# Graph kernel on one core: a shorter segment-maximum recurrence, and node blocks moved from the second graph stage beside the softmax tail of the output stage

## The reference, cut to what matters

```python
logits = w1[target] - w2[source] + d
seg_max = jax.ops.segment_max(logits, target, num_segments=m)
e = jnp.exp(logits - seg_max[target])
denom = jax.ops.segment_sum(e, target, num_segments=m)
out = jax.ops.segment_sum(e / denom[target] * (w3[source] + d), target, num_segments=m)
```

## Time and profile before

| | us |
|---|---|
| median of 3 runs (3369.0 to 3388.23) | 3370.6 |
| profiled execution | 3347.96 |
| its span, first to last instruction | 3346.2 |
| busy: PE, DVE, POOL, ACT | 2459.9, 2486.4, 1925.5, 1724.2 |

### The profile page before, as it was taken

One profiled execution on the slowest core, in us unless ns is written; L12 is line 12 of the kernel. 1 busy time (PEld: TensorE's weight loads), 2 busy tenths in 40 slices (PEclk: granted clock), 3 DMA queues, 4 the chain that ended last, 5 costly groups with the idle time before them and its releaser, 6 DMA issues. The chain is left out here.

```text
span 3346.2 us, 53978 instructions
## 1 busy us (share of the span) xinstructions
PE 2459.9 (74%) x14171; PEld 1675.7 (50%) x14171; DVE 2486.4 (74%) x4558; ACT 1724.2 (52%) x3950; POOL 1925.5 (58%) x1870
## 2 busy tenths in 40 slices
PE   3976666666578789979946779998999998995000
PEld 1543444444467667745525556665666656663000
DVE  5569999999777758859966747776566665888553
ACT  3784444444222258858841126665566655775221
POOL 4008888887488800068870047775655437886776
PEclk9988787787777888879977989998999998997555
DMA  4133333433466668733313445555445543332111
GB/s 129 64 96 87 107 99 107 109 106 98 119 199 196 191 144 180 153 104 115 112 46 75 113 127 167 157 162 159 135 136 141 139 106 108 112 114 68 47 47 27
DMA packets 742887, 393.28 MB, mean 118 GB/s; under 512 B 517090, under 2 KB 649265, under 8 KB 742770
## 3 DMA queue, kind: packets, MB, share of 16 engines
q1 hardware_dynamic: 691582, 333.94, 36.4%
q0 software_dynamic: 51200, 58.03, 6.8%
HBM read 217.18 MB, written 175.64 MB: 117 GB/s over the span
## 5 line engine op out<-in xcount | busy, mean ns | idle before, releaser
L1341 POOL DMA_INDIRECT g_W<-t,g_cols x400 | 463.2, 1158 | 260.8 <-PE g_pS L2901 116.4
L460 POOL DMA_INDIRECT fr_W<-in_x,fr_idx x400 | 496.0, 1240 | 127.6 <-issue 107.7
L1341 POOL DMA_INDIRECT me_W<-t,me_cols x200 | 236.0, 1180 | 58.0 <-issue 46.9
L1341 POOL DMA_INDIRECT ou_W<-t,ou_cols x200 | 222.6, 1113 | 58.1 <-issue 40.8
L3433 POOL DMA_INDIRECT de_V<-t,de_cols x200 | 215.8, 1079 | 53.6 <-issue 41.4
L3117 POOL DMA_INDIRECT out<-ou_F,ou_ways x200 | 200.1, 1000 | 77.5 <-issue 53.3
L1058 PE MATMUL at_pL<-at_XF,w_logit 128*128 128x512 f32 x100 | 89.7, 996 | 123.0 <-ACT at_XF L1105 123.0
L1331 POOL COPY g_cols<-pos 128x8 int32 (+1 forms) x50 | 19.8, 396 | 241.2 <-POOLq L85 241.0
L1331 POOL COPY de_cols<-pos 128x8 int32 (+1 forms) x25 | 8.1, 324 | 261.4 <-POOLq L85 261.2
L931 ACT ACTIVATE me_nzt<-me_pXT 128x512 f32<-128x512 f32 x47 | 28.1, 598 | 170.9 <-PE me_pXT L914 170.9
L914 PE MATMUL at_pXT<-ident,at_nz 128*128 128x128 f32 x200 | 40.3, 336 | 93.8 <-ACT at_nzt L931 52.3
(11 more groups left out here) (619 smaller groups left out, 8536.8 us busy)
## 6 DMA issues: line engine op xcount, KB each, us to landing
mg_y<-wanted SPq DMA_DIRECT2D x50, 256.0 KB
at_nx<-in_x SPq DMA_DIRECT2D x50, 256.0 KB, 2.6
x<-at_nz SPq DMA_DIRECT2D x50, 256.0 KB, 3.3
x1T<-at_nzt SPq DMA_DIRECT2D x50, 256.0 KB, 2.9
t<-up_X SPq DMA_DIRECT2D x100, 128.0 KB, 2.0
t<-g_HS SPq DMA_DIRECT2D x50, 256.0 KB
t<-g_HD SPq DMA_DIRECT2D x50, 256.0 KB, 3.4
g_D<-t SPq DMA_DIRECT2D x50, 256.0 KB
```

What stands on the lines that cost most here:

```text
L460: self.nc.gpsimd.indirect_dma_start(out=self.W[w][b][:, (2 * t + h) * C:(2 * t + h + 1) * C], out_offset=None, in_=self.table, in_offset=b ...
L1341: nc.gpsimd.indirect_dma_start(out=slot(w, b, t), out_offset=None, in_=table, in_offset=bass.IndirectOffsetOnAxis(ap=cols[w][:, c:c + 1], ...
```

## The change

Four parts.

1. **Attention.** The mask goes into the recurrence one edge ahead: `M = max(M_before, pL) + anew`, with `anew` read from `same` one column further on (the tile gets two more columns, set to zero). A single DVE difference `A = M_before - pL` is left. ACT makes the two exponents from it, as `L = Relu(A)` and `A = Relu(-A)`, and takes `Exp` with scale -1 of both.
2. **Node blocks.** BLOCKS_G1 is 21, gcn2_stage has none and its steps follow `by_ring`, and output_stage has 47: 25 beside its edge steps and 22 beside the tail (`LateOrder`). The order is turned round: the dense stage does blocks 0 to 28 and the last one, the output stage 50 to 96.
3. **Tail.** Each operation on G3 handles a whole step in one instruction, on 128x512. `late` weaves it between the node lane's operations. The norm is written back into G3, and POOL copies it from there into F before it scatters.
4. **Scatter.** POOL no longer waits for all node blocks, but for as many as the last target row of the step needs. That number is worked out on DVE at the head of the stage (`needed`) and loaded into a register per step. x3 is loaded by one DMA a step, the first two ahead of the stage's other loads.

```diff
-                        s.activation(anew[b][:, :], k.same[:, bass.ds((2 * q + b) * CE, CE)], ACT.Copy,
+                        s.activation(anew[b][:, :], k.same[:, bass.ds((2 * q + b) * CE + 1, CE)], ACT.Copy,
...
+                    for b in first:
+                        act.wait_ge(e["diffs"], last_of(q, b))
+                        s.activation(L[b][:, :], A[b][:, :], ACT.Relu).then_inc(e["bent"], 1)
+                        s.activation(A[b][:, :], A[b][:, :], ACT.Relu, scale=-1.0).then_inc(e["bent"], 1)
                     for b in second:
                         act.wait_ge(e["zcen"], last_of(r, b))
...
-                        v.tensor_tensor_scan(M[b][:, 1:CE + 1], anew[b][:, :], pL[b][:, :], M[1 - b][:, CE:CE + 1],
-                                             ALU.add, ALU.max).then_inc(e["maxed"], 1)
+                        v.tensor_tensor_scan(M[b][:, 1:CE + 1], pL[b][:, :], anew[b][:, :], M[1 - b][:, CE:CE + 1],
+                                             ALU.max, ALU.add).then_inc(e["maxed"], 1)
                         dve.wait_ge(e["maxed"], last_of(q, b))
+                    for b in first:
+                        v.tensor_tensor(A[b][:, :], M[b][:, 0:CE], pL[b][:, :], ALU.subtract)\
+                            .then_inc(e["diffs"], 1)
...
-                    for b in first:
-                        v.tensor_tensor(L[b][:, :], pL[b][:, :], M[b][:, 1:CE + 1], ALU.subtract)
-                        v.tensor_tensor(A[b][:, :], M[b][:, 0:CE], anew[b][:, :], ALU.add).then_inc(e["shifted"], 1)
-                    for b in first:
-                        dve.wait_ge(e["shifted"], last_of(q, b))
-                        v.tensor_tensor(A[b][:, :], A[b][:, :], M[b][:, 1:CE + 1], ALU.subtract)\
-                            .then_inc(e["diffs"], 1)
```

The counts and the scatter:

```diff
-BLOCKS_G1, BLOCKS_G2, BLOCKS_OU = 23, 22, 23
+BLOCKS_G1, BLOCKS_OU = 21, 47
+FIRST_OU = D_FULL - BLOCKS_OU
+FIRST_G1 = FIRST_OU - BLOCKS_G1
...
                 def scatter(q, w):
                     pool.wait_ge(sent, q + 1)
+                    pool.wait_ge(e["norm"], q + 1)
+                    if again(q):
+                        for b in range(2):
+                            pool.wait_ge(scattered[w][b], ring_count(q, w, 16 * CT) - 16 * CT)
+                    nc.gpsimd.tensor_copy(F[w][:, :], G3[:, bass.ds(q * (G * C), G * C)]).then_inc(copied, 1)
+                    blocks = nc.gpsimd.value_load(needed[0:1, bass.ds(q, 1)], min_val=16, max_val=16 * BLOCKS_OU)
+                    pool.wait_ge(lane.o_out, blocks)
+                    pool.wait_ge(copied, q + 1)
                     for b in range(2):
-                        pool.wait_ge(e["norm"], last_of(q, b))
...
-                beside.stored(pool)
+                pool.wait_ge(told, 8)
```

The tail on ACT and its place among the lane's operations (DVE and PE are woven alike):

```diff
+                def late(f, w, x, y, z):
+                    if x is not None:
+                        lane.act_relu(act, x)
+                        lane.act_square(act, x)
+                    if y is not None:
+                        lane.act_flat3(act, y)
+                    if z is not None:
+                        lane.act_exp(act, z)
+                    soft(f)
+                    if y is not None:
+                        lane.act_hidden(act, y)
...
+                    squares(f)
...
+                    spread(f)
+
+                beside.run_late(act, step, late)
```

More of the change, by code:

```diff
@@ L274, in _ @@
                 gp.memset(k.w_value[:, 0:C], 0.0)
+                gp.memset(k.same[:, EP:EP + 2], 0.0)
                 gp.memset(k.ones[:, :], 1.0)
@@ L2871, in step @@
                         own_rows(q + 2, w)
-                    beside.load(sp, q + 2, w)
                     store(q)
-                    beside.store(sp, q - 2, out)
                 for q in range(2):
                     own_rows(q, q, used=False)
-                    beside.load(sp, q, q)
-                beside.run_queue(sp, step)
-                beside.stored(sp)
+                with sp.Fori(0, ITERS // 2 - 1) as j:
+                    step(2 * j, 0)
+                    step(2 * j + 1, 1)
+                for q in range(ITERS - 3, ITERS):
+                    step(q, q % 2)
                 for b in range(2):
@@ L3386, in _, with top @@
-                beside.run(dve, step)
-                by_two(dve, finish)
+                part = lambda f: groups(G3[:, bass.ds(f * (G * C), G * C)], G)
+                def top(f):
+                    dve.wait_ge(e["kept"], 2 * f + 2)
+                    v.tensor_reduce(out=st[:, 0, :], in_=part(f), op=ALU.max, axis=AX).then_inc(e["max"], 1)
+                    dve.wait_ge(e["max"], f + 1)
+                    reuse(dve, e["norm"], f)
+                    v.tensor_tensor(O4, part(f), over(st[:, 0, :], C), ALU.subtract).then_inc(e["less"], 1)
@@ new lines, in by_degree, with total @@
+                def by_degree(f):
+                    dve.wait_ge(e["less"], f + 1)
+                    v.tensor_tensor(O4, O4, over(k.dinv[:, bass.ds(f * G, G)], C), ALU.mult).then_inc(e["scaled"], 1)
+                def total(f):
+                    dve.wait_ge(e["exp"], f + 1)
+                    v.tensor_reduce(out=st[:, 1, :], in_=O4, op=ALU.add, axis=AX).then_inc(e["esum"], 1)
+                    dve.wait_ge(e["esum"], f + 1)
+                    v.reciprocal(st[:, 2, :], st[:, 1, :]).then_inc(e["erec"], 1)
@@ new lines, in norm, with late @@
+                def norm(f):
+                    dve.wait_ge(e["dev"], f + 1)
+                    v.tensor_tensor(part(f), O4, over(st[:, 4, :], C), ALU.mult).then_inc(e["norm"], 1)
+                def late(f, w, x, y, z):
+                    if z is not None:
+                        lane.dve_max(dve, z)
+                        lane.dve_less(dve, z)
+                    top(f)
+                    if x is not None:
+                        lane.dve_clamp(dve, x)
+                    by_degree(f)
+                    if z is not None:
+                        lane.dve_esum(dve, z)
+                        lane.dve_recip(dve, z)
+                        lane.dve_soft(dve, z)
+                        lane.dve_mix4(dve, z, w)
+                    total(f)
+                    if x is not None:
+                        lane.dve_scale(dve, x)
+                        lane.dve_mix2(dve, x, w)
+                    mix(f, 1 - w)
+                    if z is not None:
+                        lane.dve_sumsq4(dve, z)
+                    if x is not None:
+                        lane.dve_sumsq2(dve, x)
+                    if z is not None:
+                        lane.dve_norm4(dve, z)
+                    sumsq(f)
+                    if x is not None:
+                        lane.dve_norm2(dve, x, w)
+                    norm(f)
@@ L3390, in dense_stage @@
+                v.tensor_copy(needed[:, :], whole[:, :]).then_inc(told, 1)
+                beside.run_late(dve, step, late)
 def dense_stage(nc, k, out):
```

330 lines of the change are left out of this document (157 added, 173 removed).

## The result

The changed kernel takes 3281.6 us (median of 4 runs, 3265.6 to 3292.3) against 3371.8 for the kernel before (4 runs beside them, 3369.0 to 3388.2): a ratio of 0.9715, 95% interval 0.9682 to 0.9749. Run again beside the first experiments it gave 3300.6 against 3372.8, ratio 0.9761 (0.9687 to 0.9834). The forecast of 3287 us lies between the two. The profiled execution has a span of 3263.9 us, 82.3 less than before; the sum had said 84.

The account below looks back on a forecast made before the run. It took DVE to bound attention, PE the second graph stage and scatters the old tail. Terms -29 - 4 - 133 + 2 + 80 = -84 us, taken off the runs' median 3370.6, gave 3287 us; range 3225 to 3360.

Parts of the forecast that it names:

- the sum: Whole kernel: the stage terms added up, -84 us against the profiled 3348.0 us.
- Attention, -29 forecast: Attention: four fewer DVE instructions save 2.41 us a step, a new wait costs 1.2; step 23.7 instead of 24.87.
- The walk through one step: Attention: following DVE and ACT from the scans' end, four Relus delay ACT's square and DVE waits some 1.2 us.
- Case A: Attention: POOL's gathers keep the step at 24.9 us, no gain there, total 3316 us; chance 0.15.
- gcn1, -4 forecast: First graph stage: two steps lose their node work and get 2 us shorter each; bounds 0 and 4.
- gcn2, -133 forecast: Second graph stage: without its 22 node blocks, 22 steps of 17.24 us become 11.2, paced by POOL's gathers.
- the bound of -100: Second graph stage: steps of 12.7 us if PE's clock falls with its load, a gain of only 100 us.
- Output stage, +82 forecast: Output stage: +2 us in the first part, +80 in the tail, with 22 tail steps of 13.9 us.
- the two terms: Output tail, DVE's step: 12.4 us of work plus 1.5 of waits, 13.9 us together.
- Case B: Output tail: scatters held by DVE's two-input instructions pace it at 16.5 us a step, total 3344 us; chance 0.18.
- Case C: Output tail: node and softmax chains do not overlap, 20.8 us a step, total 3438 us; chance 0.09.

Follow-up runs that it names:

- the first experiments: The first of three series of follow-up runs, with the kernel before run beside it at a median of 3372.8 us.
- the merged tail alone: The kernel before with its softmax tail's DVE and ACT instructions covering both halves of a step, no node block moved: 3379.5 us, ratio 1.0028.
- the halves: The changed kernel with each of DVE's nine softmax instructions in the tail issued as two of half the size: 3299.3 us, ratio 0.9793.
- two more copies: The changed kernel with two more 128x512 copies on POOL in each tail step, into tiles nobody reads: 3284.2 us, ratio 0.9713.
- the second execution: The changed kernel run again unchanged and profiled: 3300.6 us, ratio 0.9761; its profile is 37.1 us longer than the first.

## Why the prediction was right

**What bounds each stage.** All four readings held: DVE in attention, PE in gcn2, scatters in the old tail (shown by the merged tail alone), DVE in the new tail (shown by the halves; with two more copies POOL still kept up). For gcn2 the reading was right but one figure was not: by subtraction of the node lane's tiles, PE was to have 8.8 us a step left, and it has 10.

**Attention, -29 forecast, -34.9 measured.** The walk through one step named the new wait, its place (DVE's reduce of R) and its cause (the Relus ahead of ACT's square). Its size was 0.82 us, not 1.2: the Relus start 0.52 us apart and not 0.60. So the step gained 1.5 us instead of 1.2, and the steps after the first are the miss. Moving the Relus took the wait away, which shows the cause.

**Case A** (gathers hold attention at 24.9) is out: 23.4 in the changed kernel, 22.7 with the Relus early. POOL is busy 441 us in the stage instead of the 472 of the earlier trace rows, as its gathers are held less.

**gcn1, -4 forecast, -19.5 measured.** Mis-sized, and partly no effect of the change. "Two steps get 2 us shorter" was too little here: the last four scans (of the first half of a step) come 11.9, 12.6, 9.8 and 8.6 us apart, before 14.2, 14.0, 11.9 and 12.6, so 9.8 us less for two blocks, and what follows the last scan takes 3.5 us instead of 5.9. Another 6.2 us are two steps of the kernel before that took 17.2 us instead of 14.1, because the clock fell in them. The step before it and that step:

```profile
2090.00:2104.00 14.00, 14.00 (x90) 9.56 (x89) 10.95 (x17) 9.42 (x19) 10.95 (x10) 1.00 0.61 170
2104.00:2122.00 18.00, 18.00 (x94) 11.92 (x94) 11.38 (x19) 10.46 (x22) 9.70 (x10) 0.81 0.53 143
```

With the attention change alone there is no such step, and gcn1 takes 359.1 us instead of 365.9; the changed kernel has none in one execution and one in the other. The end of the stage varies as well: in the second execution the last two intervals are 10.6 and 12.1 us, at a granted clock of 0.87 and 0.50 (0.65 and 0.80 in the first), so the four lost only 5.5 us, near the forecast's 4. One more us was not looked into.

**gcn2, -133 forecast, -135.1 measured.** Step 11.0, not 11.2; late next was the gather, as read from the head of the old stage. PE waits for gathered tiles, as here between 2380 and 2530 us, where POOL has little but its issue gaps:

```profile
PE g_pS L2939 <- DMA g_W<-t,g_cols: 13.9, 13, 1.1
```

The clock did not fall (0.96 over the stage), so the bound of -100 was not needed. But PE's load did not fall as said either: 10.0 us of a step of 11.0, not 8.8 of 11.2. The subtraction took no account of times that overlap: the other tiles already held PE 155.4 of the 252.5 us of the earlier trace rows, 10.6 a step. By these numbers 1 us more would have made PE set the step. In the second execution the stage took 299 us, with steps of 11.4 and gathers of 1100 ns instead of 1052: 125 us less than before.

**Output stage, +82 forecast, +88.7 measured.** From the stage's start the first norm comes after 320.5 us (316.4 by the sum), then 22 steps of 14.01 in the mean (13.9), then 47.7 us to the end of the span (47.5). In the step shown above the two terms were off in opposite directions: DVE's work is 12.66 us (12.4), its waits 1.04 (1.5), and the only wait that the profile names is norm4's, 0.60. PE's part is 8.4 only at a granted clock of 1.00, and 9.9 at the usual 0.88. POOL's comes to 12.8, from its copy to the end of its last scatter (12.1). Seventeen of the 22 steps are 13.4 to 13.9; the rest are steps in which the clock was 0.77 to 0.86, or the very last, at 0.51. In the second execution the mean is 14.35, with nine steps of 14.9 to 15.8.

**Case B** (16.5 us a step) is out: scatters take 1075 ns beside ten two-input instructions. The rule that spoke for it (the Trainium skill, GPSIMD Engine Reference, Specifications: GpSimd's SBUF interfaces contend with VectorE instructions of two SBUF inputs) shows in the trace, but small. Of the 200 scatters, 76 start while such an instruction runs, and take 1.22 us in the mean; the 124 others take 0.98, none over 1.01. One of the long ones is that of 2995.20 above; it starts in this instruction:

```profile
2994.91 0.69 DVE L1630 TENSOR_TENSOR ou_E<-ou_E,ou_st 128x512 f32<-128x512 f32 x1
```

Over all it is 0.08 us a scatter, where case B had 0.55. The long ones in attention stood beside pairs of 1.28 us; here each instruction is 0.69 us long, and most scatters start beside none. **Case C** (20.8 us) is out: DVE idled 1.04 us in that step.

**What the sum left out.** Edge, dense and attention2, which the change doesn't touch, came out 18.6 us longer. They offset what attention and gcn1 gained beyond the forecast, so the total is closer to the forecast than its terms are: that the sum met the span within 2 us is luck, and the second execution missed it by 39. All three vary as much between two executions of one kernel, edge and attention2 with the clock, so nothing points to the change.

## What to carry to other kernels

Look for an engine that is full in one stage and idle in another, and move the work that the first cannot hide: a node block cost 6.2 us beside gcn2 (steps of 17.2 and 11.0 us) and 3.4 beside the tail (14.0 and 10.6), whose own scatters had to run anyway. When work is handed from one engine to another, walk the receiving queue: what stands behind the new instructions, and who waits for it, was 16 us here and cost a move of four lines to get back. Merging instructions paid 0.06 us each in the woven tail, and nothing where another engine set the pace. A copy put on GpSimd is not free for VectorE even when GpSimd has time: it lengthened 16 of the two-input instructions that started during it from 0.69 us to 0.87 or 1.17.
